# Experts over sorted tokens in place of experts over all tokens

## What is computed

```python
x = _ln(src + attn_out, ln1_g, ln1_b)
gates = softmax(xf @ gW + gb)                      # 8 experts
top2_scores, top2_idx = top_k(gates, 2)
w = (one_hot(top2_idx, 8) * top2_scores[..., None]).sum(1)
h = relu(einsum('nd,edf->enf', xf, W1) + b1[:, None, :])   # d 256, f 512
y = einsum('enf,efd->end', h, W2) + b2[:, None, :]
out = einsum('ne,end->nd', w, y)
x = _ln(x + out, ln2_g, ln2_b)
```

## Time and profile before

| | us |
|---|---|
| median of 3 runs (4839.7 to 4841.41) | 4840.15 |
| the profiled execution, its own time | 4840.44 |
| its span in the trace | 4838.7 |
| `attention_output`, 1815 to 1946 us of the span | 131 |
| `experts`, 1946 to 2693 | 747 |
| `moe_output`, 2693 to 2923 | 230 |

### The profile page before, as it was taken

The page is one execution under the profiler, slowest core; times in us unless marked ns, Lnnn a source line. Parts: engine busy times, 40 slices in busy tenths (PEclk is TensorE's granted clock), DMA queues, the critical chain, the costliest instruction groups (busy, mean ns, idle before and its releaser), DMA issues. The chain is left out here.

```text
span 4838.7 us, 64027 instructions
## 1 busy us (share of the span) xinstructions
PE 3789.2 (78%) x19288; PEld 1859.8 (38%) x19288; DVE 3722.8 (77%) x5114; ACT 2057.9 (43%) x2482; POOL 1502.2 (31%) x768
## 2 busy tenths in 40 slices
PE   4779999999999995799999637762666766646665
PEld 1413333233233325699999413320111111125554
DVE  5678888888888857554554696994898889878998
ACT  0426766666666671122222004561444344413332
POOL 0210000000000004000000131554888889844454
PEclk7969999999999997899999658885777777768887
DMA  1720110100101004200000222434111112121110
GB/s 60 238 67 4 38 37 6 38 17 24 39 3 39 3 5 136 70 18 9 9 9 0 67 98 79 145 115 128 59 56 55 54 55 64 55 66 46 43 35 13
DMA packets 214764, 254.44 MB, mean 53 GB/s; under 512 B 33992, under 2 KB 170064, under 8 KB 213328
## 3 DMA queue, kind: packets, MB, share of 16 engines
q1 hardware_dynamic: 208288, 242.29, 16.3%
q10 hardware_dynamic: 6320, 10.03, 0.6%
HBM read 142.30 MB, written 109.58 MB: 52 GB/s over the span
## 5 line engine op out<-in xcount | busy, mean ns | idle before, releaser
L856 DVE TENSOR_REDUCE att_maxima<-att_ps_m 128x1 f32<-128x512 f32 x2048 | 1281.0, 683 | 250.8 <-PE att_ps_m L899 247.1
L830 ACT ACTIVATE att_probs<-att_ps_s 128x1024 f32<-128x1024 f32 x1024 | 996.1, 1021 | 433.7 <-PE att_ps_s L913 431.0
L899 PE MATMUL att_ps_m<-att_ks,att_qs 96*128 (+1 forms) x2048 | 730.8, 393 | 46.8 <-DMA att_ks<-scratch_k 28.8
L913 PE MATMUL att_ps_s<-att_qs,att_ks 99*128 (+1 forms) x2048 | 612.9, 381 | 13.9 <-DMA att_qs<-att_m_parts 11.7
L2065 POOL TENSOR_TENSOR ss_ch<-ss_h,ss_c_rep 128x1024 f32<-128x1024 f32 x256 | 594.5, 2347 | 3.4 <-DVE ss_h L2111 3.2
L921 PE MATMUL att_ps_o<-att_probs,att_vs 128*32 128x512 f32 x4096 | 547.2, 606 | 0.4 <-ACT att_probs L830 0.4
L2086 ACT ACTIVATE ss_ps_d<-ss_ps_d,ss_a_neg 128x1024 f32<-128x1024 f32 x256 | 278.6, 1088 | 521.2 <-PE ss_ps_d L2151 521.0
L1274 ACT ACTIVATE ex_hid_whole<-ex_ps_h,ex_b 128x512 f32<-128x512 f32 x256 | 175.8, 689 | 561.8 <-PE ex_ps_h L1349 537.9
L899 PEld LDWEIGHTS att_ps_m<-att_ks,att_qs 96*128 (+1 forms) x2048 | 165.4, 97 | 641.5 <-DVE att_maxima L856 367.0
L2173 PE MATMUL ss_ps_y<-ss_ch,ss_sum_block 128*32 128x256 f32 x2048 | 211.7, 497 | 143.9 <-POOL ss_ch L2065 143.9
L2143 PE MATMUL ss_ps_x<-ss_stack,ss_spread 96*128 96x512 bf16 x512 | 196.5, 473 | 152.8 <-ACT ss_skip L2074 74.4
(11 more groups left out here) (369 smaller groups left out, 6634.0 us busy)
## 6 DMA issues: line engine op xcount, KB each, us to landing
scratch_steps<-si_parts SPq DMA_DIRECT2D x48, 512.0 KB, 6.1
ss_stack<-scratch_steps SPq DMA_DIRECT2D x256, 96.0 KB
att_qs<-scratch_q SPq DMA_DIRECT2D x192, 64.0 KB
scratch_v<-qkv_v_ext SPq DMA_DIRECT2D x8, 1024.0 KB, 4.4
att_vs<-scratch_v SPq DMA_DIRECT2D x8, 1024.0 KB
ex_w_whole<-in_W SPq DMA_DIRECT2D x16, 512.0 KB
scratch_xc<-si_xc SPq DMA_DIRECT2D x8, 1024.0 KB, 4.3
scratch_zs<-si_zs SPq DMA_DIRECT2D x8, 1024.0 KB, 4.3
```

What stands on the lines that cost most here:

```text
L830: act.activation(probs[:, (2 * kt + pair) % 4, :, :], ps_s[pair][:, :, :], ACT.Exp, scale=HD ** -0.5).then_inc(exp_done, 1)
L856: dve.tensor_reduce(maxima[:, j, c:c + 1], ps_m[BANK[j * QC + c]][:, :], AX.X, ALU.max).then_inc(maxed, 1)
L899: pe.matmul(ps_m[BANK[j * QC + c]][:, :], q, k, start=True, stop=True).then_inc(scored, 1)
L913: mm = pe.matmul(ps_s[pair][:, i, :], ks[0:ROWS, bass.ds(st // QC % 2, 1), h, kt * P:(kt + 1) * P], qs[0:ROWS, bass.ds(st // QC % 2, 1), b ...
```

## The change

The routing is turned from weights over 8 experts into places. In `attention_output`, the rank gives two one-hot tensors `chosen` (first and second expert) and the scores. PE counts, for each token, the earlier tokens of the same expert (products with a triangular and a full matrix of ones, 14 products of 8 columns and more per group), VectorE turns counts into row numbers, and GpSimd scatters each tile of xa twice into `sorted_x` in DRAM by an indirect DMA, 64 in all. Each expert has a region of 4096 + 128 rows there. After the groups, VectorE makes a table of 72 entries: which expert and which first row each tile of sorted tokens has; the table holds int32 in SBUF, and engines read it into registers. SP writes 128 zero rows behind each expert's last row. xa stays in SBUF; the two stores of xa are gone. All weights of all experts are loaded at the start of `attention_output` from ACT's queue (16 DMAs of 512 KB) and split there by VectorE, one expert per step. b1 is laid out anew in DRAM by a DMA inside `head_attention`.

`experts` has 72 units of 128 sorted tokens. `moe_output` gathers each tile's two results by 64 indirect DMAs, ACT multiplies them by the scores, and PE adds them with the identity to the same PSUM, now in two buffers. The loops of `attention_output` and `moe_output` are unrolled (`unroll=True`); those of `experts` stay hardware loops.

```diff
-def run_stages(eng, units, *stages):
+def run_stages(eng, units, *stages, unroll=False):
+REGION = T + P
+SORTED = T * 2 // P + E
@@ head_attention, SyncE, after load_quad(1, 1)
+                    sp.dma_start(scratch.b1_rows.rearrange("o (e t p) -> p (o e) t", e=E, t=FT), scratch.io["b1"]).then_inc(b1_laid, 16)
                 store_shift(0)
@@ attention_output, SyncE
-                run_stages(sp, GROUPS, (load_heads, -2), (load_src, -1), (store_xa, 1))
+                run_stages(sp, GROUPS, (load_heads, -2), (load_src, -1), unroll=True)
+                sp.wait_ge(ends_copied, 1)
+                sp.wait_ge(zero_set, 1)
+                for e in range(E):
+                    end = sp.value_load(route.ends[0:1, e:e + 1], min_val=e * REGION, max_val=e * REGION + T)
+                    sp.dma_start(scratch.sorted_x[bass.ds(end, P), :], heads[:, 0, 0, :]).then_inc(zeroed, 16)
@@ GpSimd
-                run_stages(pool, GROUPS, (add_bias, 0), (gain_shift, 1))
+                def scatter(g, slot):
+                    pool.wait_ge(placed, g + 1)
+                    for t in range(g * GT, (g + 1) * GT):
+                        for a in range(2):
+                            pool.indirect_dma_start(scratch.sorted_x[:, :], bass.IndirectOffsetOnAxis(route.slots[:, a, t:t + 1], 0),
+                                                    xa[:, t, :], None).then_inc(scattered, 16)
+                run_stages(pool, GROUPS, (add_bias, 0), (gain_shift, 1), (scatter, 5), unroll=True)
@@ VectorE
+                def split_weights(e, slot):
+                    dve.wait_ge(w_loaded[e], 2 * 16)
+                    for high, low in (route.w1, route.w2):
+                        split_high(dve, high[:, e, :, :], low[:, e, :, :].bitcast(F32)).then_inc(w_high, 1)
...
+                    dve.tensor_scalar(both[:, :, :], rank[:, :, :], 2.0, None, ALU.is_lt).then_inc(both_ready, 1)
+                    c.then(dve.tensor_tensor(route.chosen[:, :, g * GT:(g + 1) * GT, :], which[:, :, :, :], over(rank[:, :, :].unsqueeze(1), [P, 2, GT, E]), ALU.is_equal))
+                    c.wait()
+                    c.then(dve.tensor_tensor(picked[:, :, :, :], route.chosen[:, :, g * GT:(g + 1) * GT, :], over(z[:, :, :].unsqueeze(1), [P, 2, GT, E]), ALU.mult))
+                    c.wait()
+                    c.then(dve.tensor_reduce(route.scores[:, :, g * GT:(g + 1) * GT], picked[:, :, :, :], AX.X, ALU.add))
...
+                def find_places(g, slot):
+                    dve.wait_ge(counted, g + 1)
...
+                run_stages(dve, GROUPS, (find_places, 5), (shift_logits, 4), (add_src, 1), (take_best, 4), (normalise, 1), (split_weights, 2, E), unroll=True)
@@ ScalarE
+                for e in range(E):
+                    act.dma_start(route.w1[1][:, e, :, :].bitcast(F32), io["W1"][e:e + 1, :, :].rearrange("o (k p) f -> p (o k) f", p=P)).then_inc(w_loaded[e], 16)
+                    act.dma_start(route.w2[1][:, e, :, :].bitcast(F32), io["W2"][e:e + 1, :, :].rearrange("o (k p) c -> p (o k) c", p=P)).then_inc(w_loaded[e], 16)
@@ experts, SyncE
+                def load_x(m, slot):
+                    row = sp.value_load(route.table[0:1, 1, bass.ds(m, 1)], min_val=0, max_val=E * REGION - P)
+                    if third_on(m):
+                        sp.wait_ge(x_turned, m - 1)
+                    sp.dma_start(x[:, slot, :], scratch.sorted_x[bass.ds(row, P), :]).then_inc(x_loaded[slot], 16)
+                    if isinstance(m, int) and m == 1:
+                        sp.dma_start(b1[:, :], over(scratch.b1_rows, [P, E * FF])).then_inc(b_loaded, 16)
...
+                run_stages(sp, SORTED, (load_x, -2), (store_y, 3))
@@ VectorE: split_x splits the transposed tile out of PSUM, then
+                def add_b1(m, slot):
+                    e = dve.value_load(route.table[0:1, 0, bass.ds(m, 1)], min_val=0, max_val=E - 1)
...
+                    dve.tensor_tensor(hid[:, slot, :], ps_h[slot][:, :], b1[:, bass.ds(e * FF, FF)], ALU.add).then_inc(h_biased, 1)
+                def split_hidden(m, slot):
...
+                    dve.tensor_scalar(high, ps_t[slot][:, :, :], 0.0, None, ALU.max).then_inc(h_high, 1)
...
+                    dve.scalar_tensor_tensor(low, ps_t[slot][:, :, :], 0.0, high.bitcast(F32), ALU.max, ALU.subtract).then_inc(h_split, 1)
+                run_stages(dve, SORTED, (split_x, 0), (add_b1, 1), (split_hidden, 2))
@@ TensorE: turn_x makes 2 transposes, turn_hidden 4
+                def hidden(m, slot):
+                    e = expert_of(m)      # pe.value_load of the table's entry m
+                    pe.wait_ge(x_split, m + 3)
+                    pe.wait_ge(h_biased, m + 1)
+                    for k in range(KC):
+                        for i, j in SPLIT:
+                            mm = pe.matmul(ps_h[slot][:, :], x_t[i][:, slot, k, :], w1[j][:, bass.ds(e, 1), k, :].rearrange("p a f -> p (a f)"),
+                                           start=(k, i, j) == (0, 0, 0), stop=(k, i, j) == (KC - 1, *SPLIT[-1]))
...
+                def output(m, slot):
+                    e = expert_of(m)
...
+                    for f in range(FT):
+                        for i, j in SPLIT:
+                            mm = pe.matmul(ps_y[slot][:, 0, :], hid_t[i][:, slot, f, :], w2[j][:, bass.ds(e, 1), f, :].rearrange("p a c -> p (a c)"),
+                                           start=(f, i, j) == (0, 0, 0), stop=(f, i, j) == (FT - 1, *SPLIT[-1]))
+                run_stages(pe, SORTED, (turn_x, 0), (hidden, 1), (turn_hidden, 2), (output, 3))
@@ moe_output
+                def gather(g, slot):
+                    if third_on(g):
+                        pool.wait_ge(bias_ready, g - 1)
+                    for a in range(2):
+                        for t in range(GT):
+                            pool.indirect_dma_start(back[:, slot, a, t, :], None, scratch.sorted_y[:, :],
+                                                    bass.IndirectOffsetOnAxis(route.packed[:, a, g * GT + t:g * GT + t + 1], 0)).then_inc(gathered[slot], 16)
+                run_stages(pool, GROUPS, (gather, -2), (scale_y, 0), (scale_xn, 3), unroll=True)
+                def weigh(g, slot):      # ScalarE, 8 activations of 256 columns
...
                     for t in range(GT):
-                        pe.matmul(ps_b[:, t, :], gate_t[:, t * P:(t + 1) * P], b2[:, :], start=True, stop=False)
-                        mm = pe.matmul(ps_b[:, t, :], ident[:, :], xa[:, slot, t, :], start=False, stop=True)
+                        pe.matmul(ps_b[slot][:, t, :], gate_t[:, t * P:(t + 1) * P], b2[:, :], start=True, stop=False)
+                        pe.matmul(ps_b[slot][:, t, :], ident[:, :], route.xa[:, g * GT + t, :], start=False, stop=False)
+                        for a in range(2):
+                            mm = pe.matmul(ps_b[slot][:, t, :], ident[:, :], back[:, slot, a, t, :], start=False, stop=a == 1)
```

457 lines of the change are left out of this document (248 added, 209 removed).

## The result

The changed kernel takes 4530.8 us (median of 4 runs, 4526.9 to 4532.4), the one before 4839.9 beside it: a ratio of 0.9362, 95% interval 0.9346 to 0.9378. It is 309 us faster. 4640 was forecast, 200 us faster, within a range of 4490 to 4790. The sign and the range held; the likeliest number missed by 109 us, more than half of the gain that it named.

The account below looks back on a forecast made before the run. TensorE was taken to bound `experts`, VectorE `attention_output` and `moe_output`. Forecast 437 + 208 + 255, plus 8 for `head_attention`, is 908 against 1108 us: 200 less than 4840.4, so 4640 us, range 4490 to 4790.

Parts of the forecast that it names:

- both covers: GpSimd's indirect DMAs, taken at 1.4 us, hide under VectorE's steady steps up to 1.65 us each in `attention_output`, 1.8 in `moe_output`.
- the rival with 1.2 GHz: In `experts`, gaps twice a step drop the array's clock: 7.1 us a step, stage 548, total 4751 us; chance 0.12.
- the rival that ends slower: GpSimd, issuing 128 indirect DMAs, bounds `attention_output` and `moe_output`; at 4 us each the kernel takes 4971 us; chance 0.12.
- `moe_output` came within 5 us: Stage forecast: 230 us, less 7 in VectorE's steps, plus 32 for a longer start, gives 255 us.
- I take 1.0 us, uncovered: In `experts`, each of TensorE's two register loads a unit adds 1.0 us to 3.62 of array time: 5.6 us a step.
- the term for the start: In `experts`, 13 us for b1's broadcast and the loads before it, 2 for the last store: 15 us beside 75 steps.
- The sentence that gave the total by the skill's figure: In `experts`, with register loads at about 0.6 us, a step would be 4.8 us and the total 60 us lower.
- The rival with hidden loads: In `experts`, TensorE's sequencer runs ahead: step 3.6 to 4.1 us, stage 287 to 320, total 4490 to 4520; chance 0.12.
- the split of the weights: In `attention_output`, VectorE splits one expert's weights in 4.1 us with waits, eight times: 33 us.
- VectorE still without waits for GpSimd in the steady steps: Sign that the forecast holds, in `attention_output` and `moe_output`, with steady steps of 20 and 24 us.
- the end: End of `attention_output`, uncovered: counting, places, the last 8 scatters at 1.4 us and their landing, 16 us.
- The start: Start of `attention_output`: weights share DMA engines with the first heads and ACT's issues delay its copy; 10 us, between 0 and 25.

## Why the prediction was right, and where it was wrong

**Right in sign and range.** The gain comes from the experts, by fewer products at the spacings of the earlier trace rows: the array's share of a step was worked out as 3.62 us and is 3.48. The clock stayed at 1.0 in the steady steps, that is 2.4 GHz (0.97 over the stage), in spite of the gaps, so the rival with 1.2 GHz is out; with the loads tripled, and gaps of up to 2.0 us twice in most steps, it was 0.94 over the stage. The Trainium skill (TensorE: Matmul & The Clock Gate, "HAM oscillation — how this bites in real kernels") tells of a low clock from gaps that return with each tile; at the gaps of 0.35 us of this trace it did not come to that. GpSimd never bound a steady step: an indirect DMA took 1.27 us from start to start against 1.4 forecast, under both covers, so the rival that ends slower is out too. VectorE's step in the experts, priced from columns (0.42 and 0.69 us), was exact to 0.01 us an operation. `moe_output` came within 5 us. `head_attention` came within 2 in this profile; in the others with the DMA in its old place its end lies 5.8 to 14.5 us behind that of before.

**The range held by luck in part.** Its lower end, 4490, was drawn so as to leave out hidden loads with everything else at its best, and hidden, but for 0.4 us a step, is what they were. The experts' miss of 143 us alone would have brought the total to 4497, 7 us above that end; the 31 us of `attention_output`, missed the other way, made it 41.

**Wrong: the register loads.** The step of the sum that failed is "I take 1.0 us, uncovered. A step is then 3.62 + 2.0". The price was too high and, worse, the form was wrong: the loads were added to the array's time. The run with six loads gives 0.64 us each, and the run with one shows that they run beside the array: the step is the longer of the array's 3.48 us and the sequencer's 2.60 + 0.64 per load. The Trainium skill (DMA: Bandwidth & Descriptors, "Latency and other measured facts") names a floor of about 0.6 us; the 0.64 is near it only with the range check, the load by itself held the sequencer for 0.36 us. 75 x 3.88 is 291 of the 294 us, so that the term for the start, put at 15 us, is 3 on top of the steps: 131 us of the 143 are the step, 12 the start. The sentence that gave the total by the skill's figure added in the same way and came to 4.8 us a step, so the right price alone would have left more than half of this error. The rival with hidden loads named 3.6 to 4.1 us a step and 287 to 320 for the stage, which is where it lies, at a chance of 0.12. Its total of 4490 to 4520 was missed only through `attention_output`. What spoke for it was seen and underrated: before, the array ran 600 us without a gap through loops and waits, so the sequencer had slack.

**Wrong: the split of the weights.** 33 us were put down from the earlier trace rows, a stage in which GpSimd did nothing; 65.7 was measured, in a stage in which it is busy for 133 us. "VectorE still without waits for GpSimd in the steady steps" was named as a sign, and it fails in a form that no view of waits shows: VectorE waits inside its operations. The error did not come through in full: 28 us of waits on GpSimd's passes were already in VectorE's 97.9 us of before, in operations of 4 and 32 columns (their time above that of the shortest of their kind); after the change 11 us of such waits are left in small operations and 37 are in the splits, 19 more in all than before and not 35. From the first add to the table VectorE takes 174.6 us; 112 of before, 18 for routing and 33 for the splits are 163. So 12 us of the 31.

**Wrong: the end.** 16 us were forecast, 31 measured. The forecast counted the last 8 scatters only, with GpSimd's step of 18.3 us under VectorE's 20.2. That holds in a steady step, and fails at the end, where VectorE's step is 6 to 9 us and GpSimd's 10: "covered" was asked of the wrong steps. 15 us of the 31.

**The start** was priced at 10, between 0 and 25, and is 14.4 (33.6 against 19.2); the mechanism, ScalarE held by its own issues and the heads late on the shared DMA engines, is shown by the run with the weights behind the heads. 4 us of the 31.

## What to carry to other kernels

TensorE's sequencer and its array were two sums here, and a step the longer one, so count both, and cut the number of register loads rather than move them. Price an operation from a row in which the engine beside it does what it will do after the move, and look for small operations with long times: they are waits, and they pass to whatever is put in their place. Cover found in steady steps says nothing of the last ones of a pipeline; the resource that lags one step behind comes due there all at once.

## What the hardware showed beyond this

- **A register load costs more than it shows.** 0.30 us in its row, 0.36 us of TensorE's sequencer to the next row, 0.64 us with its range check.
- **A stall that no run explains.** In all profiles of the runs above, though not in the changed kernel's own, VectorE stops one to three times near the end of `attention_output`, for 3 to 17.6 us, ahead of L1225 or its like, with TensorE's counts done when the stop has just begun and a releaser that the trace calls "remote". It makes most of the difference between the 239.5 us of the one profile and the 243 to 245 of the others; of its 15 us only 4 to 5 come through, because GpSimd works off its backlog meanwhile. The trace has no packet of the instruction queue inside any of the stops, so it shows no code being fetched in them. In nine profiles VectorE went on 2.3 to 3.5 us after the end of the last scatter that GpSimd could issue (2033.7 and 2037.0 in the run with one load a step), in the other three at least one stop ended amid scatters. That the scatters hold something that VectorE waits for is only a guess; it was not tried.
- **Indirect DMAs are cheap to issue and even.** Of 128 rows of 1 KB each, most scatters took 1.27 us from start to start and most gathers 1.25; the longest, behind a pass or beside VectorE's splits, 2.36.
